# GpSimd's product with B in two instructions of 768 columns, each tied to its own half scan

## The reference, cut to what matters

```
dA  = exp(dt[..., None] * A)
dBu = dt[..., None] * Bm[:, :, None, :] * u[..., None]
h   = dA_t * h + dBu_t                    # for every step t of a sequence
y   = einsum('bdn,bn->bd', h, C_t)
```

## Time and profile before

| what | value |
|---|---|
| time, median of 3 runs | 1898.82 us (1897.49 to 1899.72) |
| the profiled execution | 1895.89 us |
| its span | 1893.7 us |
| what lies around the span | 2.2 us |
| busy in the span: PE, DVE, POOL, ACT | 1500.1, 1382.1, 1086.9, 871.8 us |

### The profile page before, as it was taken

How to read it: one execution, slowest core, us unless ns; L and a number is a source line. 1 busy time by engine, 2 the same in 40 slices (tenths; PEclk the granted TensorE clock), 3 DMA queues, 4 the chain that set the end, 5 groups by cost and what they waited for, 6 DMA issues and landing times. The chain is left out here.

```text
span 1893.7 us, 21043 instructions
## 1 busy us (share of the span) xinstructions
PE 1500.1 (79%) x5318; PEld 888.2 (47%) x5319; DVE 1382.1 (73%) x1548; ACT 871.8 (46%) x1946; POOL 1086.9 (57%) x636
## 2 busy tenths in 40 slices
PE   5777877888688678768878777888572799999997
PEld 3433344445344344434444444444242466666665
DVE  4399999998998999899899989998977122222221
ACT  2465545655464565556555545655531122222221
POOL 2376686767758576776676676766740233333333
PEclk8789898998899899889989998999885899999999
DMA  3402122240313124041313312131202634343332
GB/s 86 159 30 105 71 90 83 67 159 19 131 52 110 56 92 150 10 145 37 125 40 108 108 53 101 48 133 58 92 1 83 238 83 91 84 90 88 84 90 51
DMA packets 60428, 165.71 MB, mean 88 GB/s; under 512 B 17086, under 2 KB 29100, under 8 KB 60364
## 3 DMA queue, kind: packets, MB, share of 16 engines
q1 hardware_dynamic: 48220, 148.91, 22.8%
q0 software_dynamic: 12144, 16.13, 4.7%
HBM read 152.98 MB, written 12.03 MB: 87 GB/s over the span
## 5 line engine op out<-in xcount | busy, mean ns | idle before, releaser
L635 POOL TENSOR_TENSOR ring<-dtu,brep 128x1536 f32<-128x1536 f32 x192 | 666.5, 3473 | 377.5 <-DVE states L646 337.7
L658 PE MATMUL py<-ring,ident 128*128 128x384 f32 x1536 | 608.8, 541 | 231.9 <-ACT yg L671 146.1
L646 DVE TENSOR_TENSOR_SCAN states<-states,ring 128x768 f32<-128x768 f32 x384 | 674.2, 1756 | 87.7 <-ACT states L622 72.3
L658 PEld LDWEIGHTS py<-ring,ident 128*128 128x128 f32 x1536 | 303.3, 208 | 507.1 <-issue 156.0
L622 ACT ACTIVATE states<-dt_,aneg 128x376 f32<-128x376 f32 x768 | 405.8, 559 | 0.1
L648 DVE TENSOR_TENSOR ring<-states,crep 128x768 f32<-128x768 f32 x384 | 367.6, 957 | 13.2
L619 ACT ACTIVATE states<-zero_cols 128x16 f32<-128x16 f32 x384 | 70.0, 182 | 514.1 <-DVE ring L648 508.9
L1364 DVE COPY yidx<-place 128x1 int32 (+1 forms) x56 | 8.4, 153 | 246.2 <-DMA out_tokens<-ys,yidx 246.2
L1291 POOL DMA_INDIRECT xs<-x_scratch,yidx x56 | 55.3, 987 | 227.5 <-DVE yweight L1370 149.5
L1318 PE MATMUL gu<-w,xsT 128*128 x440 | 155.2, 496 | 5.5 <-issue 4.9
L467 PE MATMUL pf<-xT,wxz 97*128 97x384 f32 (+1 forms) x384 | 142.5, 509 | 16.1 <-ACT xT L454 8.2
(11 more groups left out here) (228 smaller groups left out, 1561.2 us busy)
## 6 DMA issues: line engine op xcount, KB each, us to landing
brep<-b_c_rows SPq DMA_DIRECT2D x64, 768.0 KB, 3.9
crep<-b_c_rows SPq DMA_DIRECT2D x64, 768.0 KB, 5.9
rest<-in_w_rest SPq DMA_DIRECT2D x55, 384.0 KB, 3.2
w<-in_w SPq DMA_DIRECT2D x8, 768.0 KB, 8.5
wd<-in_wd SPq DMA_DIRECT2D x8, 576.0 KB, 9.3
ptok<-in_p_tok SPq DMA_DIRECT2D x8, 384.0 KB, 3.6
pT<-in_p_T SPq DMA_DIRECT2D x8, 384.0 KB, 4.3
out_tokens<-h SPq DMA_DIRECT2D x8, 288.0 KB, 2.1
```

The lines of the kernel that those rows point to most:

```text
L635: gp.tensor_tensor(ring[:, w % NRING], dtu[:, d, o, :].unsqueeze(1).to_broadcast([128, GN, T]), brep[:, ng], ALU.mult).then_inc(dbu_ok, 1)
L646: v.tensor_tensor_scan(h_in, h_in, x_in, 0.0, ALU.mult, ALU.add).then_inc(scan_ok, 1)
L658: mm = pe.matmul(py[:, 0:T], ident[:], ring[:, w % NRING, i, :], start=(ng == 0 and i == 0), stop=False)
```

## The change

The product with B becomes two instructions of 768 columns, one for each half of the unit. The second waits for the second half scan of the unit two back, where the whole product waited for the first one only. DVE waits for `dbu_ok` ahead of each half scan, not once in a unit; as the semaphore now counts halves, the other two readers' numbers are doubled.

```
-                wait(act, dbu_ok, UD * (e - 1))
+                wait(act, dbu_ok, 2 * UD * (e - 1))
...
-                wait(sp, dbu_ok, last_use)
+                wait(sp, dbu_ok, 2 * last_use)
...
-            wait(gp, scan_ok, 2 * (U - AHEAD) + 1)
-            gp.tensor_tensor(ring[:, w % NRING], dtu[:, d, o, :].unsqueeze(1).to_broadcast([128, GN, T]), brep[:, ng], ALU.mult).then_inc(dbu_ok, 1)
+            for i in range(2):
+                wait(gp, scan_ok, 2 * (U - AHEAD) + 1 + i)
+                part = slice(HALF * i, HALF * i + HALF)
+                gp.tensor_tensor(ring[:, w % NRING, part], dtu[:, d, o, :].unsqueeze(1).to_broadcast([128, HALF, T]), brep[:, ng, part], ALU.mult).then_inc(dbu_ok, 1)
...
-            v.wait_ge(dbu_ok, U + 1)
             v.wait_ge(crep_in[ng], 16 * (e + 1))
             for i in range(2):
+                v.wait_ge(dbu_ok, 2 * U + i + 1)
```

## The result

The changed kernel takes 1904.27 us (median of 7 runs, 1903.65 to 1906.44). The kernel before took 1897.14 us in the 7 runs beside it (1895.40 to 1899.72). The ratio is 1.0038, 95% interval 1.0027 to 1.0049: slower by 7.1 us, where 18 were forecast. The profiled execution took 1904.27 us, its span 1902.4.

The account below looks back on a forecast made before the run. DVE was taken to bound the Mamba stretch, busy 92% of it. Steps 12, embedding 1 and reduction 5 made 18 us on a profiled 1895.9, so 1914; with the median's 2.9, 1917; forecast 1916, range 1899 to 1922.

Parts of the forecast that it names:

- The half's size: POOL's product of 768 columns was to take 1.81 us, bounds 1.72 and 2.0.
- Steps: Slots' two-input DVE work (L576, L579) waits for the later second half: 13 places of 0.84 us, two of about 0.5; 12 us.
- Embedding: L396 on DVE ends some 0.15 us later behind the second half, 7 times: 1 us.
- Reduction: Slot 3: four halves take turns with L361, L363 and two L367; 9.7 us against 8.99, 5 us in seven chunks.
- rivals 1: Reduction: DVE's next instruction goes ahead of the waiting half, so each reduction meets one half only; 1881 us, faster; 8%.
- Rival 2: Reduction: L367 passes POOL without waiting, making it 6 to 17 us shorter; 1894 to 1906 us; 17%.
- The split wait on DVE: DVE's added semaphore wait in each unit was to cost zero; 10 us were it 0.05 us in the open each time.
- Rival 4: The split wait shows on DVE, 18 + 10 us: 1924 to 1928 us; 5%.
- The first scan: It can start 1.6 us sooner on half a product; gain put at nothing, bounds 0 and 1.6 us.
- The median: The runs' median was put 2.9 us above the profiled execution, taking 1914 us to 1917.
- rival 3: The delays vanish in the scans' waits for ACT, leaving 0 to 6 us: 1897 to 1903 us; 12%.
- The idle time ahead of the scans: Sign on DVE: to stay near 88 us with ACT as main cause; a fall would speak for rival 3.

Follow-up runs that it names:

- e3: The changed kernel with both halves of the product released by the first half scan two units back: 1893.21 us.
- e8: e1 with DVE's reduction in slot 4, one slot later, and the sines left in slot 5: 1856.36 us.
- e1: The kernel before with 48 one-column memsets of an unread tile ahead of DVE's loop, moving its code by 48 instructions: 1888.47 us.
- e2: The changed kernel with 80 one-column memsets of an unread tile ahead of DVE's loop, so that it touches four blocks again: 1919.88 us.
- e5: e1 with the reduction moved from slot 3 to slot 5 and the sines from slot 5 to slot 6: 1881.77 us.
- e4: The kernel before with the whole product released by the second half scan two units back, no instruction added or moved: 1966.87 us.

## Why the prediction came out as it did

**The sign was right, the size was wrong**: plus 18 forecast, plus 7.1 measured.

- The half's size: 1.81 us undisturbed, mean 1856 ns with the blocked ones. Right. The estimate worked out from the Trainium skill's "GPSIMD Engine Reference" (section 3.1), 1.69 us, was too short here.
- Steps: forecast 12, measured 12.0; 0.84 us at 13 places, about 0.5 at the two others. e3 shows that the later release causes it. Right.
- Embedding: forecast 1, measured 0.7, in this arrangement of the queues. The sum is right in part by luck: chunks 0 and 1 gave 0.35 and 0.19, the five others 0.02 to 0.03 each, where 0.15 in each of seven was forecast.
- Reduction: forecast 5, measured 3.9 over slots 1 to 5. The pattern is as told (L361 and L363 2.45 us, L367 1.78), so rivals 1 and 2 fall: L367, with one tensor from SBUF, waits as the others do (356 ns a piece in e8, without POOL beside it). Of this the Trainium skill's "SBUF — State Buffer" (Who interferes with whom) says that a DVE instruction with at most one SBUF input doesn't contend with GpSimd, save in the two-port modes, which it names for this operation among others; which mode L367 ran in no run here shows. One detail was off: L359 was to take 1 us and took 1.66, as the product dtu (L630) ran ahead of the halves. The sum of 3.9 is near to 5 by luck. The forecast took 8.99 us of chunk 3 for all seven chunks, but before the change (from L359's start to the end of the second L367) only chunks 3 to 6, behind a stalled jump, took 8.9 to 9.1; chunks 0 to 2 took 9.9 to 10.0. After it, six took 10.4 to 10.5 and chunk 0 9.1: in the four 1.4 us more, twice the 0.7, and in the three together nothing. And in the four, some 1.4 us came back as a shorter wait for ACT ahead of slot 3 (1.81 us for 3.1 to 3.3). That belongs to the moved code, as e1 has the shorter wait too, and reductions of 10.0 to 10.2 us in those chunks. In chunk 3, the kernel before, then e1:

```profile
602.69 1.76 DVE L646 TENSOR_TENSOR_SCAN states<-states,ring 128x768 f32<-128x768 f32 x1 [3.16 <-ACT states L622]
```

```profile
600.60 1.76 DVE L647 TENSOR_TENSOR_SCAN states<-states,ring 128x768 f32<-128x768 f32 x1 [1.67 <-ACT states L623]
```

- The split wait on DVE: zero. POOL ends 1.0 us of the scans' idle time. Rival 4 falls as far as waiting goes.
- The first scan: it came 1.39 us sooner, and the next unit's scan then waited 3.04 us for ACT where it had waited 0.51, so slot 0 lost 2.5. Nothing gained, as forecast; against the kernel before it is a loss of 1.1, against e1 a gain of 0.3.
- **The step that failed is the sum.** It added the terms to the time of before as if nothing else could move. "Zero; were it 0.05 us in the open" priced DVE's added wait as a wait, and never as an instruction that takes room in the program. The row that held the missing term was quoted: 9.9 us of "issue" ahead of the scans. The prediction named ACT's 72.3 and POOL's 4.7 from that row and passed over the third cause, so the moved code stood in the sum at nothing. It was worth 10.2 us at the four jumps; by e1 and e2, moving the code alone is worth 8.6 us of time on the kernel before and 15.6 on the changed one.
- The median: 2.9 us were added from three runs. Over more runs the kernel before stands at 1897.1, 1.2 above its profiled execution. That is the other 1.7 us. 1916 less 10.2 less 1.7 is 1904.1. That this meets 1904.3 so closely is luck in part: the three terms came 1.4 short of 18, and 1.8 came from the first scan, slot 0 and the other slots, which stood at nothing.
- Rival 2's sum is wrong in itself: it takes the 6 and 17 us off 13 and not off 18. That makes +12 to +1, so 1900 to 1911 where it says 1894 to 1906. The measured time lies in both, yet L367 waited, so this rival is not what happened.
- The idle time ahead of the scans was to stay near 88 us, and its fall was to speak for rival 3. It fell to 74.8, and yet rival 3 is wrong: ACT's part fell by 2.0 only, and in e2, which has the stall again, the change costs more than forecast. A sign that two causes can give tells nothing until the row is split by cause.

## What to carry to other kernels

An edit that adds instructions to a loop's engine, or ahead of its loop, moves the loop's code, and that alone was worth 8.6 us here on one kernel and 15.6 on the other: before a small difference is put down to the edit's idea, look at "issue" time behind the jump and at the packets of the instruction queue, and give both kernels the same placement. Where POOL and DVE exclude each other, ask of each two-input instruction what POOL has on its queue at that moment; moving one group of five instructions by a slot was worth 32 us, where the cut of the products cost 15.8 with like placement. A group moved so late that its readers wait gives most of the gain back, as e5 shows.

## What the runs showed of the hardware

- A loop of 289 DVE instructions (291 in the changed kernel, 18 KB) stayed resident over its iterations when it began at instruction 6 or 38 of a block of 128, and was refetched with five packets of 8 KB an iteration when it began at 110, 118 or 122. A refetch held the scan behind the jump for 2.4 to 2.7 us in the kernel before, 4.0 in the mean in e4; why longer there is not shown. The starts are worked out with one inferred offset; that two borders lie between 4 and 16 and between 48 and 120 added instructions is measured. The five packets fit four blocks and one fetched ahead.
- The Trainium skill's "Runtime: NRT & Kernel Launch" (Instruction fetch mechanics) says that a taken branch whose target isn't in the current window of two pages forces a fetch before execution goes on, with blocks of 16 KiB and 32 KiB in all for most engines. The stall at the jump agrees. The block size does not, and here the measurement decides: the packets of this queue were of 8 KB, and a loop that lay in three of them was not fetched again at all. Four blocks of 8 KB make the page's 32 KiB; that a loop of three and one fetched ahead just fits is an estimate from that figure.
